# A 16-head cross-attention stage with its chunk loop written out, fixed work banks, four turned tiles ahead, and the bias row summed on GpSimd

## The reference, cut to what matters

```python
def _cross_attention(q_in, kv_in, wq, bq, wk, bk, wv, bv, wo, bo, bias_k, bias_v):   # H=16, K=128, D=512
    qh = (q_in @ wq + bq).reshape(b, q_len, H, K)
    kh = (kv_in @ wk + bk).reshape(b, t, H, K)
    vh = (kv_in @ wv + bv).reshape(b, t, H, K)
    kh = jnp.concatenate([kh, broadcast(bias_k, (b, 1, H, K))], axis=1)   # one extra key
    vh = jnp.concatenate([vh, broadcast(bias_v, (b, 1, H, K))], axis=1)   # and its value
    logits = jnp.einsum('bqhk,bthk->bhqt', qh, kh) / sqrt(K)
    ctx = jnp.einsum('bhqt,bthk->bqhk', softmax(logits), vh).reshape(b, q_len, H * K)
    return ctx @ wo + bo

x = x + _cross_attention(layer_norm(x), ctx, ...)    # weights 1
x = x + _cross_attention(layer_norm(x), ctx, ...)    # weights 2
x = x + mlp(layer_norm(x))
```

## Time and profile before

| what | value |
|---|---|
| median of 3 runs | 4874.15 us (4868.62 to 4882.09) |
| the profiled execution | 4869.24 us, span 4867.5 us |
| busy PE, PEld | 4233.3 us (87%), 3114.2 us (64%) |
| busy DVE, ACT, POOL | 2751.3 (57%), 2057.1 (42%), 919.2 (19%) us |
| mean granted clock of PE | 0.942 |
| the chain that ended last | PE 69%, DVE 10%, issue 10%, ACT 5%, POOL 3% |

### The profile page before, as it was taken

How to read it: one execution, slowest core, us unless ns; L and a number is a source line. 1 busy time by engine, 2 the same in 40 slices (tenths; PEclk the granted TensorE clock), 3 DMA queues, 4 the chain that set the end, 5 groups by cost and what they waited for, 6 DMA issues and landing times.

```text
span 4867.5 us, 65883 instructions
## 1 busy us (share of the span) xinstructions
PE 4233.3 (87%) x21794; PEld 3114.2 (64%) x21794; DVE 2751.3 (57%) x4340; ACT 2057.1 (42%) x3512; POOL 919.2 (19%) x908
## 2 busy tenths in 40 slices
PE   6799799997999987888877996999979999778988
PEld 5555477776777766554665555777767777655446
DVE  2477555555555553666424785555565555537664
ACT  2377434333443432555223773344333443324642
POOL 1421212211121113100214212122121221130002
PEclk9899899998999988999888998999989999889989
DMA  1200101100110012000212001011010110110002
GB/s 62 54 18 10 44 24 39 33 21 30 33 39 23 30 32 59 18 2 0 69 69 56 17 10 48 20 39 36 18 39 24 39 34 19 37 56 15 2 6 72
DMA packets 151556, 157.87 MB, mean 32 GB/s; under 512 B 14021, under 2 KB 118666, under 8 KB 151442
## 3 DMA queue, kind: packets, MB, share of 16 engines
q1 hardware_dynamic: 143762, 146.96, 9.7%
q0 software_dynamic: 7680, 9.45, 1.2%
HBM read 144.84 MB, written 2.10 MB: 30 GB/s over the span
## 4 chain that ended last, share of the span: by engine, by line
PE 69%; DVE 10%; issue 10%; ACT 5%; POOL 3%; DVEq 1%; DMA 1%; ACTq 0%; POOLq 0%; SPq 0%
PE ps L146 18%; PE ps L148 16%; PE ps L147 16%; PE ps L1692 3%; PE ps L1333 3%; PE ps L904 2%; DVE w_pt_lo L1838 2%; PE ps L1321 2%; PE ps L886 2%; PE ps L916 2%; PE ps L1345 2%; ACT w_pt_hi L1764 1%; DVE w_v_lo L1833 1%; POOL g_qs L1258 1%; DVE l_pt L1056 1%
## 5 line engine op out<-in xcount | busy, mean ns | idle before, releaser
L1838 DVE TENSOR_TENSOR w_pt_lo<-ps,w_pt_hi 128x512 fp32r<-128x512 f32 x512 | 349.5, 687 | 238.3 <-ACT w_pt_hi L1764 238.3
L1764 ACT ACTIVATE w_pt_hi<-ps 128x512 fp32r<-128x512 f32 x512 | 301.3, 595 | 388.6 <-PE ps L1692 388.6
L1460 DVE CUSTOM_DVE_ANT_0 g_units<-ps,g_mask 128x1024 f32<-128x1024 f32 x256 | 312.0, 1219 | 143.1 <-PE ps L1321 101.8
L1821 DVE TENSOR_REDUCE w_mx<-ps 128x1 f32<-128x1024 f32 x256 | 312.6, 1221 | 79.6 <-PE ps L148 79.6
L1625 POOL CAST w_wo_hi<-w_raw 128x1024 fp32r<-128x1024 f32 x32 | 33.2, 1037 | 1592.3 <-PE ps L148 1592.3
L146 PE MATMUL ps<-w_pt_hi,w_v_hi 128*128 128x512 f32 x512 | 243.0, 475 | 93.8 <-DVE w_pt_lo L1838 84.4
L1405 ACT ACTIVATE g_units<-g_units,g_nmx 128x1024 f32<-128x1024 f32 x256 | 294.5, 1150 | 54.8 <-DVE g_nmx L1460 51.8
L1692 PE MATMUL ps<-ident,w_p 128*128 128x128 f32 x2048 | 309.0, 274 | 0.0
L1333 PE MATMUL ps<-ident,g_units 128*128 128x128 f32 x2048 | 292.2, 286 | 7.6 <-ACT g_turned L1413 5.7
L1333 PEld LDWEIGHTS ps<-ident,g_units 128*128 128x128 f32 x2048 | 227.2, 145 | 110.6 <-issue 66.9
L1692 PEld LDWEIGHTS ps<-ident,w_p 128*128 128x128 f32 x2048 | 255.3, 141 | 65.0 <-issue 2.8
(11 more groups left out here) (374 smaller groups left out, 10812.6 us busy)
## 6 DMA issues: line engine op xcount, KB each, us to landing
w_raw<-in_L_xattn_wk SPq DMA_DIRECT2D x32, 512.0 KB, 3.4
w_raw<-in_L_xattn_wq SPq DMA_DIRECT2D x32, 512.0 KB, 3.4
w_raw<-in_L_xattn_wv SPq DMA_DIRECT2D x32, 512.0 KB, 3.6
w_raw<-in_L_xattn_wo SPq DMA_DIRECT2D x32, 512.0 KB, 3.3
mlp_raw<-in_L_xattn_w_fc SPq DMA_DIRECT2D x64, 256.0 KB, 2.8
mlp_raw<-in_L_xattn_mlp_w SPq DMA_DIRECT2D x64, 256.0 KB, 2.8
ctx_nat<-in_ctx SPq DMA_DIRECT2D x4, 1024.0 KB, 13.2
g_mask<-in_mask_Bx1xSxS_ff SPq DMA_DIRECT2D x2, 2048.0 KB, 9.9
```

Of the source, the lines that this page charges most:

```text
L1460: dve.tensor_tensor_reduce(units[:, q % U, :].rearrange("p (h w) -> p h w", h=2), ps[:, 2 * (q % 2):2 * (q % 2) + 2, :], mask[:, q % 4, :] ...
L1764: act.activation(pt.h[:, tn % 4, :], ps[:, T_BANK + tn % 2, :], ACT.Copy).then_inc(turn_hi, 1)
L1821: dve.tensor_reduce(mx[:, u, lt:lt + 1], ps[:, S_BANK + 2 * (sn % 2):S_BANK + 2 * (sn % 2) + 2, :], AX.XY, ALU.max).then_inc(max_own, 1)
L1838: dve.tensor_tensor(pt.l[:, tn % 4, :], ps[:, T_BANK + tn % 2, :], as_f32(pt.h[:, tn % 4, :]), ALU.subtract).then_inc(turn.freed(tn), 1)
```

## The change

In `wide` the eight chunks are written out in all engine streams (`for c in range(C)`, no `Fori`), and the steps follow one text `order` in which what ACT does (`e` exponentials, `vh`, `th`) and what DVE does (`m` maximum, `v`, `vl`, `th`) have places of their own. Work banks are assigned by a table. The step `c` is gone from PE; POOL multiplies wo by bias_v and sums the products in `row`, and a matrix of ones adds up its partitions at the end of the stage. The `o.1` steps of the first chunk are left out. Four turned tiles of head 0 come ahead of `pv.0.0`, and those of head 1 begin within head 0's products. The tail signals DVE after each `o`. In `grouped`, `ring_free` is replaced by waits for the semaphores of the work itself.

```diff
-            for x in (("k", 0, 0), ("k", 0, 1), ("q", 0), ("k", 1, 0), ("x", 0), ("s", 0, 0), ("o", 1, 0), ("s", 0, 1),
-                      ("o", 1, 1), ("k", 1, 1), ("s", 0, 2), ("o", 1, 2), ("q", 1), ("s", 0, 3), ("o", 1, 3), ("x", 1),
-                      ("s", 1, 0), ("v", 0), ("s", 1, 1), ("vlo", 0), ("v", 1), ("s", 1, 2), ("vlo", 1),
-                      ("s", 1, 3), ("v", 2), ("vlo", 2), ("t", 0, 0), ("v", 3), ("t", 0, 1), ("vlo", 3)):
...
+            A, BB = 0, 1
+            banks = {("k", 0, 0): A, ("k", 0, 1): BB, ("q", 0): A, ("k", 1, 0): BB, ("x", 0): A, ("o", 1, 0): BB,
+                     ("o", 1, 1): A, ("k", 1, 1): BB, ("o", 1, 2): A, ("q", 1): BB, ("o", 1, 3): A, ("x", 1): BB,
+                     ("v", 0): A, ("v", 1): BB, ("v", 2): A, ("v", 3): BB, ("pv", 0): A, ("pv", 1): BB,
+                     ("o", 0, 0): A, ("o", 0, 1): A, ("o", 0, 2): A, ("o", 0, 3): A}
...
+            order = lines("""
+                k.0.0 k.0.1 q.0 k.1.0 x.0
+                s.0.0 m.0.0 e.0.0 o.1.0 s.0.1 m.0.1 e.0.1 o.1.1 k.1.1 s.0.2 m.0.2 e.0.2 o.1.2 q.1 s.0.3 m.0.3 e.0.3
+                o.1.3 x.1
+                s.1.0 m.1.0 e.1.0 v.0 vh.0 s.1.1 vl.0 m.1.1 e.1.1 v.1 vh.1 s.1.2 t.0.0 vl.1 th.0.0 m.1.2 e.1.2
+                v.2 vh.2 s.1.3 t.0.1 t.0.2 vl.2 th.0.1 m.1.3 th.0.2 e.1.3 v.3 vh.3 t.0.3 vl.3 th.0.3 rz.0
+                pv.0.0 t.0.4 th.0.4 pv.0.1 t.0.5 th.0.5 pv.0.2 t.0.6 th.0.6 pv.0.3 t.0.7 th.0.7 pv.0.4 pv.0.5
+                t.1.0 th.1.0 pv.0.6 t.1.1 th.1.1 pv.0.7 a.0 t.1.2 th.1.2 pv.1.0 pv.1.1 t.1.3 th.1.3
+                o.0.0 pv.1.2 t.1.4 th.1.4 o.0.1 t.1.5 th.1.5 pv.1.3 o.0.2 t.1.6 th.1.6 pv.1.4 t.1.7 th.1.7 o.0.3
+                rz.1 pv.1.5 pv.1.6 pv.1.7 a.1""")
+            steps = [(c,) + x for c in range(C) for x in order if c or x[:2] != ("o", 1)]
...
             def pool_(pool, b):
...
-                with pool.Fori(0, C) as c:
+                pool.memset(row[:, :], 0.0).then_inc(row_clear, 1)
+                pool.wait_ge(row_loaded, r * 16 + 16)
+                for c in range(C):
...
+                        pool.tensor_tensor(lo, raw_of(i, name), as_f32(hi), ALU.subtract)
+                        pool.drain()
+                        pool.tensor_tensor(raw_of(i, name), raw_of(i, name),
+                                           cols[:, c_xv + 2 * c:c_xv + 2 * c + 2].unsqueeze(2).broadcast_to([P, 2, D]),
+                                           ALU.mult)
+                        for h in range(2):
+                            pool.drain()
+                            pool.tensor_tensor(row[:, :], row[:, :], raw_of(i, name)[:, h, :], ALU.add)
+                        pool.drain().then_inc(split[name], 1)
...
-                        elif x[0] == "c":
-                            pe.wait_ge(split["o"], g + 2)
-                            pe.wait_ge(xv_done, g + 1)
-                            ring.wait_free(pe, g, m)
-                            for h in range(2):
-                                i = mm3(pe, bank(m)[0:1, :], xv[:, h:h + 1], w["o"][:, h, :], h == 0, h == 1)
-                            i.then_inc(ring.full, 1)
...
+                pe.wait_ge(row_done, r + 1)
+                pe.matmul(ps[:, T_BANK, :], ones[:, :], row_p.h[:, :], start=True, stop=False)
+                pe.matmul(ps[:, T_BANK, :], ones[:, :], row_p.l[:, :], start=False, stop=True)
+                pe.wait_ge(lo_done, r * n_hi + hi_of[C - 1, ("a", 1)] + 1)
                 for lt in range(LT):
                     i = mm3(pe, ps[:, S_BANK + lt, :], att[:, lt * P:(lt + 1) * P], w["o"][:, 1, :], True, True)
-                i.then_inc(last_full, 1)
+                    i.then_inc(last_full, 1)
...
                 for lt in range(LT):
+                    dve.wait_ge(last_full, r * LT + lt + 1)
+                    if lt == 0:
+                        dve.drain()
                     dve.scalar_tensor_tensor(out=X[:, lt, :], in0=ps[:, S_BANK + lt, :], scalar=rz[:, 1, lt:lt + 1],
                                              in1=X[:, lt, :], op0=ALU.mult, op1=ALU.add)
```

More of the change, by code:

```diff
@@ L1179, in grouped @@
             ring = ps[:, W_BANK, :]
[L1181 to L1184, removed]
+            ring_in = {q: [] for q in range(STEPS + TAIL)}
+            ring_jobs = [("q", 0)]
             for c in range(C + 1):
@@ new lines, in lines @@
+            def lines(text):
+                return [tuple(int(y) if y.isdigit() else y for y in x.split(".")) for x in text.split()]
+            order = lines("""
[8 more added lines that the diff above has]
+                rz.1 pv.1.5 pv.1.6 pv.1.7 a.1""")
@@ new lines, in wide @@
+            steps = [(c,) + x for c in range(C) for x in order if c or x[:2] != ("o", 1)]
+            work, per_bank, turns, hi_of, xo_of = {}, [0, 0], {}, {}, {}
+            last_in, ahead_of = [None, None], {}
+            for s_ in steps:
+                c, x = s_[0], s_[1:]
+                key = x[:2] if x[0] == "pv" else x
+                if key in banks and (c, key) not in work:
+                    bk = banks[key]
+                    work[c, key] = (bk, per_bank[bk])
+                    per_bank[bk] += 1
+                    ahead_of[c, key], last_in[bk] = last_in[bk], (c, key)
+                if x[0] in "xo":
+                    xo_of[c, x] = len(xo_of)
+                if x[0] == "t":
+                    turns[c, x[1], x[2]] = len(turns)
+                if x[0] in "kqa":
+                    hi_of[c, x] = len(hi_of)
@@ L1567, in wide @@
+            n_turns, n_hi, n_xo = len(turns), len(hi_of), len(xo_of)
+            n_s = C * 2 * LT
+            full = [sem(f"{tag}_bank_full{i}") for i in range(2)]
+            xo_done = sem(tag + "_xo_done")
+            hi_done, lo_done = sem(tag + "_hi_done"), sem(tag + "_lo_done")
+            t_full, t_hi, t_free = (sem(tag + n) for n in ("_turn_full", "_turn_hi", "_turn_free"))
+            s_full, s_free = sem(tag + "_score_full"), sem(tag + "_score_free")
             max_own, max_done = sem(tag + "_max_own"), sem(tag + "_max_done")
-            v_hi, v_done = sem(tag + "_v_hi"), sem(tag + "_v_done")
+            v_sum, v_hi, v_done = (sem(tag + n) for n in ("_v_sum", "_v_hi", "_v_done"))
@@ L1576, in wide @@
-            last_use = {"k": job["k", 1, 1], "q": job["q", 1], "v": job["v", 3], "o": job["o", 1, 3]}
-            credits.extend([ring, turn, score])
-            extra_credits.extend(list(split.values()) + [cv_done])
-            done = new_barrier()
-            bank = lambda m: ps[:, R_BANK + m % 2, :]
+            rows_loaded, row_loaded = sem(tag + "_rows_loaded"), sem(tag + "_row_loaded")
+            cv_done, row_clear, xk_done = (sem(tag + x) for x in ("_cv_done", "_row_clear", "_xk_done"))
@@ new lines, in wide, with upto, bank, wait_freed @@
+            row_done, last_full = sem(tag + "_row_done"), sem(tag + "_last_full")
+            done = new_barrier()
+            def upto(eng, s, n):
+                if n > 0:
+                    eng.wait_ge(s, n)
+            def bank(c, key):
+                return ps[:, R_BANK + work[c, key][0], :]
+            def wait_freed(eng, r, c, key):
+                if key[0] in "xo":
+                    eng.wait_ge(xo_done, r * n_xo + xo_of[c, key] + 1)
+                elif key[0] == "v":
+                    eng.wait_ge(v_sum, (r * C + c) * 4 + key[1] + 1)
+                else:
+                    eng.wait_ge(lo_done, r * n_hi + hi_of[c, ("a", key[1]) if key[0] == "pv" else key] + 1)
@@ L1582, in view, with wait_bank, wait_full @@
+            def wait_bank(eng, r, c, key):
+                if ahead_of[c, key]:
+                    wait_freed(eng, r, *ahead_of[c, key])
+            def wait_full(eng, r, c, key):
+                bk, n = work[c, key]
+                eng.wait_ge(full[bk], r * per_bank[bk] + n + 1)
             def view(name):
@@ L2029, in pe_ @@
                 for lt in range(LT):
-                    pe.matmul(ps[:, lt, :], ones_row[:, :], browp.h[:, :], start=True, stop=False, skip_group_check=True)
-                    pe.matmul(ps[:, lt, :], ones_row[:, :], browp.l[:, :], start=False, stop=False,
+                    pe.matmul(ps[:, lt, :], ones[0:1, :], browp.h[:, :], start=True, stop=False, skip_group_check=True)
+                    pe.matmul(ps[:, lt, :], ones[0:1, :], browp.l[:, :], start=False, stop=False,
                               skip_group_check=True)
```

507 lines of the change are left out of this document (230 added, 277 removed).

## The result

The changed kernel takes 4718.72 us (median of 4 runs, 4717.30 to 4721.12) against 4873.67 us; the ratio is 0.9672, 95% interval 0.9657 to 0.9688. The profiled execution took 4721.12 us with a span of 4719.3, so the span is 148.1 us shorter.

A forecast was written before the change was run, and what follows sets the result against it. PE was taken to set the pace in the attention chunks. Terms summing to 144.8 us, taken from the profiled 4869.24, gave 4724.4, or 4729 as median; own range 4700 to 4750, whole range 4665 to 4795.

The forecast's parts named there:

- The path: Attention chunks: PE sets the pace; its 4.76 us of idle time and any matmul removed can be won.
- Step `c` and the banks: PE, each chunk: six matmuls gone save 1.40 us (44.8 in all); fixed banks save 1.56 before next key (43.7).
- Table load: ACT, first key of every chunk: one load per stage instead of 32 in all; 0.56 us a chunk, 17.9 saved.
- Turned tiles: Head 0's products: loss falls from 3.8 to 3.1 us a chunk, t.0.5 waiting behind th.0.3; 22.4 us saved.
- the walk along the chain: Maxima, exponentials and low parts in head 0, followed step by step: t.0.5 starts near 836.4 at the latest.
- The bound of 1.4 us lost: Head 0's products: lower bound of the loss per chunk if POOL is never in the way, against 3.1 forecast.
- Second half: pv.0.7 to the next key: about 12.2 us of work plus 0.43 waiting, 12.65 against 12.66; no further term.
- First chunk and end: Each stage: first chunk without four `o` steps saves 2.1 us (8.4 in all), earlier additions at the end 1.9 (7.6).
- POOL: POOL's added product and additions, 5.5 to 5.9 us a chunk: cost nothing, except through DVE.
- POOL holds DVE: Rival, head 0: POOL's added work holds vl.0 and vl.1, t.0.5 at 838.4; 64 us back, 4793; chance 0.17.
- The clock: Rival, waits before t.0.5: every chunk pays 1.62 us for a stretch at 1.2 GHz; 52 us lost, 4781; chance 0.08.
- Late instructions: Rival, written-out loops: instructions must be fetched; at 2.4 us per block 95 us slower, 4969; chance 0.04.

The follow-up runs named there:

- e7_key_waits: Changed kernel with banks A and BB exchanged for steps k.0.0 to x.1, so the first key again shares pv.1's bank: 4768.96 us, ratio 0.9785.
- e6_no_c: Kernel before the change without the step c (bias row missing from its output): 4825.92 us, ratio 0.9903.
- e5_unrolled: Kernel before the change with only its five loops written out: 4858.81 us, ratio 0.9974.
- e2_no_row: Changed kernel without POOL's product and both additions for the bias row (bias_v contribution missing from output): 4708.78 us, ratio 0.9654.
- e10_splits_late: Changed kernel, but POOL splits wk, wq and wv of the next chunk only after head 0's whole product: 4645.92 us, ratio 0.9528.
- e4_turn_first: Changed kernel with t.0.3 and th.0.3 moved ahead of vh.3 and vl.3: 4674.50 us, ratio 0.9588.

## Why the prediction was right, point by point

**The path.** PE sets the pace, and its waits and matmuls were what could be won: right. A chunk has three parts:

| part | before | forecast | after |
|---|---|---|---|
| first key to pv.0.0 (two tiles more) | 45.12 | 45.26 | 45.11 |
| pv.0.0 to pv.0.7 | 11.50 | 10.80 | 10.35 |
| pv.0.7 to the next key | 16.32 | 12.65 | 12.23 |
| chunk | 72.93 | 68.7 | 67.69 |

**The sum.** A chunk gave 1.0 us more than forecast, in 28 chunks 29 us, and a stage's last chunk 2.5 us more, 10 in all; eight more stretches at 1.2 GHz took 12 back. That is about the 29 us of the first table. Longer normalizations and other stages took nearly as much, so the total is better than its parts.

**Step `c` and the banks.** 2.96 us a chunk together were forecast. The key follows in 0.23 us, and in `e7_key_waits` the bank part comes back at the size forecast (1.57 for 1.56). `e6_no_c` shows that the split between the two terms holds for this order only.

**Table load.** Right in cause (4 instead of 32, with nothing but the loops changed) and in size within what `e5_unrolled` can tell (16.4 against 17.9, interval 8 to 18).

**Turned tiles.** The wait named, t.0.5 behind th.0.3, is the one in the trace. 2.65 us are lost (10.35 - 7.7) and not 3.1; the term was 0.45 too small. The step that was off in size is the walk along the chain: it put t.0.5 at 836.4, 5.04 us behind pv.0.0, and it came 4.71 behind (822.33 - 817.62). The inside of the chain differed too: vl.1 had been given 0.6 to 0.7 us and took 2.16, vl.3 1.75 and took 1.37. The bound of 1.4 us lost with POOL never in the way was too high. With the three splits late, pv.0.0 to pv.0.7 takes 8.33 us, so 0.6 are lost, though vl.0 still meets POOL.

**Second half.** 12.2 us of work plus 0.43 of wait were estimated, 12.23 came, with a wait of 0.25 in it.

**First chunk and end.** A stage's first chunk lost 7.2 us, some 2 more than the others, as forecast (2.1); the end 7.7 for 7.6.

**POOL.** "Nothing, except through DVE" was right about POOL's own queue and incomplete about DVE. The product takes 1.90 us and not 2.37, additions 1.3 to 1.6. Within chunks leaving the work out gains next to nothing (`e2_no_row`). But the prediction looked only at chunks and put the normalizations at nothing. One assumption that failed is that `wo` of the first chunk stays where it was. Its release had been a side effect of the ring, and without the ring it fell into the normalization, in which PE is busy for 4.2 us and DVE for 17 to 31. Another is that writing the loops out leaves POOL's first split in its place (4.6 us in `e5_unrolled`). The normalizations grew by 14.7 us in all, unforeseen.

**POOL holds DVE.** As a rival to the forecast, that the row would cost 64 us, it fell. As a mechanism it is the largest thing left in this kernel: 73 us by `e10_splits_late`, all of it from the splits of wk, wq and wv that were there before the change. The sum came near because one of its two ways to t.0.5 took vl.3's held length from the trace of before, and the other started late enough without a hold; that of vl.1 was in neither. The Trainium skill, SBUF — State Buffer, "SBUF: two separate sides", states that a DVE operation with two SBUF inputs and a GpSimd operation that reads SBUF exclude each other for a whole instruction. The trace agrees: vl.3 took 2.60 us beside an instruction of 2.37, and 0.69 alone.

**The clock.** The rival priced every chunk at 1.62 us; 13 of 32 pay 1.49, 8 more than before, so 12 us. With t.0.5's wait cut from 2.00 us to 0.69 and 0.62 the stretches are gone (`e4_turn_first`, `e10_splits_late`), so both gained more than their waits. The idle time of a chunk alone does not tell when a stretch comes: before, 4.76 us of it went with 5 stretches, after, 2.67 with 13. What does was not shown.

**Late instructions.** The instruction queue moved 145 blocks instead of 64, and inside the four attention stages no wait of PE is put down to issue: no loss. The rival's 2.4 us was not the longest wait for issue in the trace of before, as the prediction has it; one of 6.1 us stands outside these stages.

**What stays open.** The 11 us in other stages. Most of it lies behind the last attention stage: from its last low part of `att` to the end pass 677.7 us before and 685.0 after, 138.2 and 152.0 of them at 1.2 GHz, though the stage's own end got 1.9 us shorter. But ten traces have the same code there. In five it takes 677.4 to 678.3 us (127.8 to 138.0 at 1.2 GHz), in five 683.5 to 685.6 (148.4 to 155.3). So about 7 of the 11 us differ from one profiled execution to the next. What decides it was not tried.

## What to carry to other kernels

When a loop is written out or a ring taken away, list what each engine had been released by, at the edges too: a side effect may have kept two engines apart. Look for DVE instructions whose length varies at one shape: here 0.69 against up to 2.60 us named the culprit, and moving GpSimd's work in time, not making it less, was worth nearly half as much as the whole rewrite (73 against 155 us). When a run gives back the amount that was lost, see whether each place went back too: here 15.2 us came for 14.7, at other places.

## What the runs showed of the hardware

- DVE differences that read two operands from SBUF were held by GpSimd instructions, large or small: 128x512 took up to 2.70 us in the kernel after and 0.69 alone, 128x16 took 1.86 beside GpSimd's product and 0.18 without. A cast of 128x16 with one operand took 1.98 beside a GpSimd difference and 0.17 without, and the normalization's scaling (four of 128x512) 5.02 instead of 1.92.
- Others that read SBUF were not held in the kernel after: the 128x1 scaling of the maximum (0.21 us in 112 cases with GpSimd running) and the statistics of the normalization (2.47 for four). Differences with one operand in PSUM kept 0.68 to 0.69.
- Such held time counts as busy: DVE's busy time fell by 1.86 us a chunk with the same instructions.
- GpSimd's product of 1024 elements with an operand repeated 512 times took 1.90 us, less than its difference of two full operands (2.40).
- Waits of 0.41 and 2.00 us in head 0 of a chunk came with stretches of 3.4 us at 1.2 GHz in 13 of 32 chunks, 1.49 us each; waits of 0.56 and 0.69 us came with none (`e4_turn_first`).
